# A causal convolution moved from four matrix products to VectorE, one broadcast comparison, and a reordered slot in a two-layer kernel

## The reference

```python
# layer 2, mixer (b = 4, L = 1024, D = 128, 16 states, 4 taps)
x_ssm, gate = split(xn @ W_in + b_in)
xc = silu(depthwise_causal_conv(x_ssm, conv_w) + conv_b)      # 4 taps along the tokens
B, C = split(xc @ W_x + b_x)
h_t = exp(-exp(A_log)) * h_{t-1} + xc_t * B_t                  # scan over tokens
y_t = C_t . h_t + D * xc_t
s   = (y * silu(gate)) @ W_out + b_out
# layer 2, feed-forward: only the upper half of the tokens by score
scores = xn @ w_router; the top 512 of 1024 are updated, weight sigmoid(score)
out = xn.at[top].add(weight * (gelu(xn[top] @ W1 + b1) @ W2 + b2))
```

## Time and profile before

| | us |
|---|---|
| median of 3 runs | 588.61 |
| the three runs | 587.46, 588.61, 590.74 |
| the profiled execution | 590.46 |
| its span, first to last instruction | 588.7 |
| PE busy | 483.9 (82%) |
| DVE busy | 406.8 (69%) |
| POOL busy | 386.1 (66%) |
| ACT busy | 291.5 (50%) |
| TensorE clock granted, mean | 0.942 of full |

### The profile page before, as it was taken

The page is one execution under the profiler, slowest core; times in us unless marked ns, Lnnn a source line. Parts: engine busy times, 40 slices in busy tenths (PEclk is TensorE's granted clock), DMA queues, the critical chain, the costliest instruction groups (busy, mean ns, idle before and its releaser), DMA issues.

```text
span 588.7 us, 6019 instructions
## 1 busy us (share of the span) xinstructions
PE 483.9 (82%) x1891; PEld 280.4 (48%) x1891; DVE 406.8 (69%) x637; ACT 291.5 (50%) x468; POOL 386.1 (66%) x373
## 2 busy tenths in 40 slices
PE   0427878988999889998999899989997999685682
PEld 0214645744565546554655565545654565231220
DVE  2453033768679688967796879796778778759683
ACT  3415664756374646473756365545756544332300
POOL 1714652797487767878686868784887688644553
PEclk9998998999899999998999899979999999896985
DMA  8300000000000010001000000001000000000000
GB/s 326 146 2 1 1 1 19 2 0 0 19 1 1 0 55 0 2 0 44 12 1 1 36 19 0 1 1 37 1 1 1 19 0 1 1 18 1 5 14 18
DMA packets 5793, 11.81 MB, mean 20 GB/s; under 512 B 896, under 2 KB 1664, under 8 KB 5504
## 3 DMA queue, kind: packets, MB, share of 16 engines
q1 hardware_dynamic: 4608, 9.47, 4.4%
q10 hardware_dynamic: 1152, 1.93, 0.9%
HBM read 9.30 MB, written 2.10 MB: 19 GB/s over the span
## 4 chain that ended last, share of the span: by engine, by line
PE 56%; DVE 17%; ACT 13%; issue 6%; POOL 4%; DMA 1%; SPq 0%; POOLq 0%; DVEq 0%; ACTq 0%
PE bank0a L854 16%; PE bank1a L934 6%; PE ybank L997 5%; PE bank1d L972 5%; DVE hs L1250 5%; PE bank0a L965 4%; PE xbank L983 3%; DVE xbank L1238 3%; DVE plain L1149 2%; PE bank0d L827 2%; PE bank1d L959 2%; PE bank1a L919 2%; DVE beats L1212 2%; ACT plain L584 2%; PE ybank L993 1%
## 5 line engine op out<-in xcount | busy, mean ns | idle before, releaser
L497 POOL TENSOR_TENSOR hs<-hs,Ct 128x512 f32<-128x512 f32 x128 | 168.5, 1319 | 28.3 <-DVE hs L1250 23.1
L1238 DVE TENSOR_TENSOR xbank<-xbank,Bt 128x512 f32<-128x512 f32 x128 | 88.2, 689 | 34.6 <-PE xbank L983 34.1
L983 PE MATMUL xbank<-xpair,spr 128*128 128x512 f32 x128 | 77.6, 608 | 32.7 <-DVE hs L1250 32.6
L470 POOL TENSOR_TENSOR hidAl<-plain,hidAh 128x512 fp32r<-128x512 f32 x48 | 62.6, 1305 | 55.7 <-ACT hidAh L585 36.0
L470 POOL TENSOR_TENSOR hidBl<-plain,hidBh 128x512 fp32r<-128x512 f32 x48 | 62.2, 1296 | 41.6 <-ACT hidBh L585 30.4
L1250 DVE TENSOR_TENSOR_SCAN hs<-decay,carry,xbank 128x512 f32<-128x512 f32 x64 | 81.9, 1279 | 7.8 <-DVE xbank L1238 0.5
L584 ACT ACTIVATE plain<-bank0a,col 128x512 f32<-128x512 f32 x64 | 44.0, 688 | 86.5 <-PE bank0a L854 86.4
L1250 DVE TENSOR_TENSOR_SCAN hs<-decay,xbank 128x512 f32<-128x512 f32 x64 | 78.0, 1219 | 4.9
L854 PE MATMUL bank0a<-hidAh,hTh 128*128 128x512 f32 x128 | 57.2, 447 | 5.5 <-POOL hidAl L470 2.7
L983 PEld LDWEIGHTS xbank<-xpair,spr 128*128 128x128 f32 x128 | 25.0, 195 | 69.5 <-DVE hs L1250 43.2
L854 PE MATMUL bank0a<-hidBh,hTh 128*128 128x512 f32 x128 | 56.8, 444 | 1.3 <-ACT hidAh L585 1.0
(11 more groups left out here) (162 smaller groups left out, 980.2 us busy)
## 6 DMA issues: line engine op xcount, KB each, us to landing
xt<-x_tok SPq DMA_DIRECT2D x8, 256.0 KB, 2.6
xr<-x_feat SPq DMA_DIRECT2D x8, 256.0 KB, 7.6
out<-xr SPq DMA_DIRECT2D x8, 256.0 KB, 2.0
fh<-h_w SPq DMA_DIRECT2D x1, 1024.0 KB, 10.1
hs<-h_w SPq DMA_DIRECT2D x1, 1024.0 KB, 11.9
lw<-l_w ACTq DMA_DIRECT2D x1, 640.0 KB, 6.4
g<-spread ACTq DMA_DIRECT2D x1, 512.0 KB, 5.5
Bt<-w_in SPq DMA_DIRECT2D x1, 512.0 KB, 7.7
```

The costliest lines, as they stand in the source:

```text
L470: pool.tensor_tensor(low[:, m, :], plain[:, k % NPLAIN, :], high[:, m, :].bitcast(F32), ALU.subtract).then_inc(hidden_low, 1)
L497: pool.tensor_tensor(h, h, Ct[:, hs_(u)], ALU.mult).then_inc(p_ready, 1)
L983: pe.matmul(xbank[i % 2][:], spr[:, at, :], xpair[:, half, hs_(u)], start=True, stop=True).then_inc(xs_full, 1)
L1238: dve.tensor_tensor(xbank[i % 2][:], xbank[i % 2][:], Bt[:, hs_(u)], ALU.mult).then_inc(xb_ready, 1)
```

## The change

1. PE makes one product for the convolution, W_in with the unshifted input (`project("conv", ...)`), in slot 4. `w_conv`, its load `conv_rows`, the three further products and the small edge products are gone.
2. ACT copies the bank times the last tap into `xc` in slot 4 (`start_taps`), in even units also the last three columns into `z_last`. DVE adds the three other taps from the bank in slot 5, behind its scan (`convolve` on DVE), each step waiting for the one before, then the edge: one small addition in even units, three small ones in odd units. Only then does ACT apply silu, in place, and count `conv` as done.
3. The four comparisons with the other half become one `TENSOR_TENSOR` of 128x2048 with broadcast operands (`compare_other`).
4. DVE's slot 0 runs the scan ahead of `residual_l0`. `low_x` goes from slot 6 to slot 7, and the unit's first `spread_x` from the start of PE's slot 7 to the end of it.

```diff
+def conv_steps(t):
+    return t // 2 * (TAPS + 2 * (TAPS - 1)) + t % 2 * TAPS
...
+            def start_taps(t):
+                if t >= 2:
+                    act.wait_ge(yg_ready, t - 1)
+                act.wait_ge(l1_act_full, done(L1_ACT, ("conv", t)))
+                last = act.activation(xc[:, hs_(t)], bank1a[:], ACT.Copy, scale=scale("conv_w", TAPS - 1))
+                if t % 2 == 0:
+                    last = act.activation(z_last[:], bank1a[:, HALF - TAPS + 1:], ACT.Copy)
+                last.then_inc(taps_started, 1)
+
             def convolved(t):
-                if t == 0:
-                    act.wait_ge(b_conv_step, 5)
-                    act.wait_ge(w_conv_ready, 1)
-                if t >= 2:
-                    act.wait_ge(yg_ready, t - 1)
-                take1(("conv", t), xc[:, hs_(t)], ACT.Silu, bias=b_conv[:, 0:1])
+                act.wait_ge(conv_step, conv_steps(t + 1))
+                act.activation(xc[:, hs_(t)], xc[:, hs_(t)], ACT.Silu, bias=b_conv[:, 0:1]).then_inc(l1_act_done, 1)
...
+                    elif s == 4:
+                        start_taps(n)
                     elif s == 5:
                         convolved(n)
...
-                    if u_next is not None:
+                    if u_next is not None and k_next > 0:
                         spread_x(u_next, k_next)
...
                         if s == 4:
-                            convolve(n, (3, 2, 1, 0))
+                            project("conv", n, W_IN[:, 0:P])
...
                         elif s == 8:
                             score_column(n)
+                    if u_next is not None and k_next == 0:
+                        spread_x(u_next, k_next)
...
+            def convolve(t):
+                dve.wait_ge(taps_started, t + 1)
+                at = conv_steps(t)
+                for i in range(1, TAPS):
+                    if i > 1:
+                        dve.wait_ge(conv_step, at + i - 1)
+                    dve.scalar_tensor_tensor(xc[:, t % 2 * HALF + i:t % 2 * HALF + HALF], bank1a[:, 0:HALF - i],
+                                             scale("conv_w", TAPS - 1 - i), xc[:, t % 2 * HALF + i:t % 2 * HALF + HALF],
+                                             ALU.mult, ALU.add).then_inc(conv_step, 1)
+                at += TAPS - 1
+                if t % 2 == 0:
+                    dve.wait_ge(conv_step, at)
+                    dve.tensor_tensor(xc[:, 0:TAPS - 1], xc[:, 0:TAPS - 1], b_edge[:], ALU.add).then_inc(conv_step, 1)
+                    return
+                for i in range(1, TAPS):
+                    dve.wait_ge(conv_step, at + i - 1)
+                    dve.scalar_tensor_tensor(xc[:, HALF:HALF + i], z_last[:, TAPS - 1 - i:],
+                                             scale("conv_w", TAPS - 1 - i), xc[:, HALF:HALF + i],
+                                             ALU.mult, ALU.add).then_inc(conv_step, 1)
...
-                if not 0 <= j < CPH:
-                    dve.tensor_scalar(bt, row, s_i, None, ALU.is_le if j < 0 else ALU.is_lt).then_inc(beats_ready, 1)
-                    return
...
+                dve.tensor_tensor(beats[:, CPH:], row.broadcast_to([P, CPH, HALF]), s_i.broadcast_to([P, CPH, HALF]),
+                                  ALU.is_le if u % 2 else ALU.is_lt).then_inc(beats_ready, CPH)
...
                 if n is not None:
-                    if s == 0:
-                        residual_l0(n)
-                    elif s == 2:
+                    if s == 2:
                         stats_l1(n)
-                    elif s == 6:
+                    elif s == 7:
                         low_x(n)
                 if u is not None:
                     scan(u, k)
+                if n is not None:
+                    if s == 0:
+                        residual_l0(n)
+                    elif s == 5:
+                        convolve(n)
```

More of the change, by code:

```diff
@@ L195, in program @@
         spr = sb("spr", [P, NGRP // 2, P], F32R)
-        w_conv = sb("w_conv", [P, TAPS, P])
+        z_last = sb("z_last", [P, TAPS - 1])
         b_taps = sb("b_taps", [P, TAPS])
@@ L539, in _ @@
             pool.tensor_scalar(earlier[:, HALF - P:HALF], tri, TINY, None, ALU.mult).then_inc(earlier_ready, 1)
-            pool.tensor_tensor(w_conv[:], lw[:, 0:P].rearrange("p (o d) -> p o d", o=1).broadcast_to([P, TAPS, P]),
-                               raw_conv, ALU.mult).then_inc(w_conv_ready, 1)
             for p in PERIODS:
@@ L919, in project @@
                     pe.matmul(bank[:], w, ynT[:, t % NYNT, :], start=True, stop=True).then_inc(l1_act_full, 1)
-                def convolve(t, taps):
-                    if TAPS - 1 in taps:
-                        open1a(("conv", t))
-                        pe.wait_ge(l1_act_done, done(L1_ACT, ("xnT", t)))
-                        if t == 0:
-                            pe.wait_ge(w_conv_ready, 1)
-                            pe.wait_ge(b_conv_step, 5)
-                    for k in taps:
-                        s = TAPS - 1 - k
-                        if s > 0 and t % 2 == 1:
-                            pe.matmul(bank1a[:, 0:s], w_conv[:, k, :], ynT[:, (t - 1) % NYNT, HALF - s:HALF],
-                                      start=False, stop=False)
-                        last = pe.matmul(bank1a[:, s:HALF], w_conv[:, k, :], ynT[:, t % NYNT, 0:HALF - s],
-                                         start=(s == 0), stop=(k == 0))
-                        if s == 0 and t % 2 == 0:
-                            pe.matmul(bank1a[:, 0:TAPS - 1], ident[:], b_edge[:], start=False, stop=False)
-                    if 0 in taps:
-                        last.then_inc(l1_act_full, 1)
                 def project_x(job, t, w):
@@ L1218, in compare, with compare_other @@
                                          ALU.subtract, ALU.is_lt).then_inc(beats_ready, 1)
+            def compare_other(u):
+                other = u // 2 * 2 + 1 - u % 2
+                dve.wait_ge(l1_act_done, done(L1_ACT, ("score_col", other)))
+                if u > 0:
+                    full1(("rank", u - 1))
+                s_i = scol[:, u // 2 % 2, cs_(other)].rearrange("p (c o) -> p c o", o=1)
+                row = srow[:, hs_(u)].rearrange("p (o i) -> p o i", o=1)
+                dve.tensor_tensor(beats[:, CPH:], row.broadcast_to([P, CPH, HALF]), s_i.broadcast_to([P, CPH, HALF]),
+                                  ALU.is_le if u % 2 else ALU.is_lt).then_inc(beats_ready, CPH)
             def token_weights(t):
@@ L1287, in slot @@
                 if t is not None:
-                    for pos in range(CH):
-                        if compare_slots(t)[pos] == s:
-                            compare(t, pos)
+                    if compare_slots(t)[CPH] == s:
+                        compare_other(t)
                     if s == weights_slot(t):
```

16 lines of the change are left out of this document (8 added, 8 removed).

## The result

| | before | after |
|---|---|---|
| median, us (4 executions of each, taken together) | 589.67 | 614.18 |
| lowest and highest | 587.46, 590.74 | 613.85, 615.01 |
| profiled span | 588.7 | 612.1 |
| TensorE clock granted, mean of that span | 0.942 | 0.914 |

The changed kernel is slower: ratio 1.041, 95% interval 1.038 to 1.043. The forecast was 610.6 us, with a range of 593 to 620.

A forecast was written before the change was run, and what follows sets the result against it. PE is busiest on average, but DVE's queue sets the pace in slots 1 to 5, where the convolution stands. Terms 6.6 + 2 + 12 + 2.5 - 1 = 22 us on 588.6 gave 610.6 us, range 593 to 620.

The forecast's parts named there:

- residual to gate: Stretch of a unit from DVE's `residual_l0` to PE's `gate`; predicted to grow 6.6 us, plus 2 for edge operations.
- gate to next: Stretch from PE's `gate` to the next unit's residual; predicted 12 us of clock loss over units 1 to 6.
- the comparison's -1: One broadcast comparison in slot 10 takes 2.5 us a unit instead of 3.05; counted as -1 us (-2 to +4).
- The `gate` path: `gate` waits for DVE's taps and ACT's silu: 1.35 us later in unit 4, 6.6 us in the sum.
- edge operations: Small DVE edge operations of the convolution, delayed beside POOL: 0.25 us per unit, 2 us, bounds 0 and 8.
- PE's idle time at `gate`: PE stands idle before `gate`: 3.9 us in unit 4; as a sign, 3 to 4.5 us in units 1 to 6.
- PE's work: PE's busy time over the kernel falls by about 20 us while the span grows.
- The clock: PE's clock falls after the new wait at `gate`: 2 us in each of units 1 to 6, 12 us, bounds 0 and 20.
- The rival without a further fall: PE's clock falls no further, only the later `gate` and the rest remain: 588.6 + 10 = 599 us; chance 20%.
- The first spreading product: Moved behind the score, it delays DVE's slot 8: 2.0 us in unit 7, 0.5 in unit 0, 2.5 us in sum.
- The scan ahead of the residual: DVE's 1.28 us scan in slot 0 fits in its wait for PE, but PE is late next: 0 us.
- the 1.79 us wait of slot 3: PE's wait for DVE's scan in unit 4, with 1.7 us lost to the clock; the new wait comes in addition.

The follow-up runs named there:

- e1: Kernel before with only the one broadcast comparison in place of four: 587.53 us, ratio 0.998 to the kernel before.
- e5: Changed kernel with 20 filler products on PE ahead of the `gate` product in units 0 to 6: 600.33 us, ratio 1.020 to the kernel before.
- e4: Changed kernel with the first spreading product back at the start of PE's slot 7: 610.89 us, ratio 1.037 to the kernel before.
- e3: Kernel before with only `low_x` in slot 7 and the first spreading product at the end of PE's slot 7: 589.77 us, ratio 1.001.
- e2: Kernel before with only the slot 0 scan ahead of the residual: 587.00 us, ratio 0.997 to the kernel before.

## Why the prediction was right, point by point

The sum was right for the most part by its mechanism and in part by luck. The terms behind it: residual to gate 6.5 us where 6.6 and 2 were predicted, gate to next of units 0 to 6 13.2 where 12 were, unit 7 3.75 where 2 were, and the comparison's -1 can't be seen apart (e1: -1.5 us by the ratio, with an interval that reaches 0). The 2 us too many and the terms that were too small leave 1.4 us between the forecast's 22.1 and the 23.5.

- **The `gate` path.** Predicted: 6.6 us in the sum for residual to gate, and 2 more for edge operations. Measured: 6.5 with the edges in it. The three taps took 2.29 us (2.28 predicted). ACT's silu took 0.72 (0.62 taken from L694), the edge 0.34 in unit 4 (0.20) and 1.10 us in odd units (0.60). Of the units, 2, 3, 4 and 6 lost 1.95, 2.06, 1.59 and 1.59, a little more than the 1.35 and 1.5; units 1, 5 and 7 lost less than the 0.35 or gained (-0.60, 0.15, -0.33). In units 1 and 5 this is because the kernel before had its own clock fall in that place.
- **PE's idle time at `gate`.** Predicted 3.9 us in unit 4 and 3 to 4.5 as a sign in units 1 to 6; measured 4.91 in units 1, 2, 4 and 6 and 5.56 in units 3 and 5, all above the sign. The taps started 3.24 us after the convolution product in the kernel after, where the prediction had 337.41 - 334.53 = 2.88. Of this the product came 0.37 us earlier, counted from the residual (15.52 against 15.89): PE's wait grew by it and the lateness did not. The longer edge and silu added 0.24 us, and PE was through with its own part 0.41 us sooner (1.81 us behind the product's start, 2.22 predicted).
- **PE's work.** Predicted 20 us less busy time, measured 14.4: products at the lower clock are longer (`gate` 2.07 us for 1.13), and that is counted as busy.
- **The clock.** Predicted 2 us for each of units 1 to 6, 12 us, bounds 0 and 20. Gate to next grew by 2.3, 1.5, 2.2, 1.6, 2.3, 1.6 and 1.7 us in units 0 to 6, 13.2 in all. e5 takes the falls away behind `gate` and gives 12.5 to 13.9 us. The rival without a further fall (599 us) is close to what e5 made, 600, but e5 has falls too, in slot 3.
- **The first spreading product.** Predicted 2.5, 2.0 of it in unit 7. e4 shows 3.3 us by the medians, 2.2 by the ratios, and 2.8 us in unit 7, up to half of it clock. Alone (e3) it shows nothing, so the price, worked out on the kernel before, holds only in the kernel after.
- **The comparison** took 2.4 us a unit (2.5 predicted; 2.27 where nothing held it up), and e1 is within 2 us of the kernel before. The price on POOL, 13 us off the path, was not foreseen.
- **The scan ahead of the residual.** Predicted 0, e2 shows -0.3%, about 2 us.
- **A wrong sign in a detail.** I expected the fall behind the 1.79 us wait of slot 3 to stay and the new one to be added. In the kernel after the wait is still there (1.78 us at 339.11) and the clock stays at 1.00 until 345. One fall took the other's place and was longer: the time missing at full clock between 135 and 460 us grew from 10.2 to 15.3 us. That the sum still fits is luck: the old falls stood ahead of `gate` and are in the first column. With them gone `gate` should have come earlier there; instead the longer chain took their place, and units 1 and 5 came out about even.

## What to carry to other kernels

Work taken from the busiest engine counts only where that engine doesn't then wait for it: here 2.4 us a unit of PE's products were exchanged for a chain ACT, DVE, ACT behind another engine's queue, and PE was idle for 4.9 us a unit. Price the idle time twice, once as lateness and once as clock, and look for a stretch that is the same in all units as a gauge, which keeps the two apart. Work moved forward into a wait is only in part a gain when it stood between jobs that hand one bank to each other: those jobs need it between them as much as the wait did.
